# Causal attention scores two heads at a time in the two halves of the array's rows

## What is computed

```python
# second layer, attention: 16 heads of 8, no mask
scores = jnp.einsum('bhqd,bhkd->bhqk', q, k) / jnp.sqrt(jnp.float32(HEAD))
attn = jax.nn.softmax(scores, axis=-1)
ctx = jnp.einsum('bhqk,bhkd->bhqd', attn, v)
# second layer, inside its feed-forward part: 16 heads of 4, causal
q = _rope(split(c @ wq), pos)
k = _rope(split(c @ wk), pos)
scores = jnp.einsum('bhqd,bhkd->bhqk', q, k) / jnp.sqrt(jnp.float32(HD))
causal = jnp.tril(jnp.ones((s, s), bool))
scores = jnp.where(causal, scores, -jnp.inf)
attn = jax.nn.softmax(scores, axis=-1)
o = jnp.einsum('bhqk,bhkd->bhqd', attn, v)
```

## Time and profile before

| what | value |
|---|---|
| median of 3 runs | 2163.86 us (2159.7 to 2165.2) |
| the profiled execution's own time | 2163.9 us |
| its span, first to last instruction | 2162.0 us |
| PE busy | 2038.4 us, 94% |
| DVE busy | 1485.4 us, 69% |
| ACT busy | 1215.9 us, 56% |
| POOL busy | 294.9 us, 14% |
| granted clock of PE, mean | 0.968 |

### The profile page before, as it was taken

How to read it: one execution, slowest core, us unless ns; L and a number is a source line. 1 busy time by engine, 2 the same in 40 slices (tenths; PEclk the granted TensorE clock), 3 DMA queues, 4 the chain that set the end, 5 groups by cost and what they waited for, 6 DMA issues and landing times.

```text
span 2162.0 us, 33753 instructions
## 1 busy us (share of the span) xinstructions
PE 2038.4 (94%) x11936; PEld 944.3 (44%) x11936; DVE 1485.4 (69%) x2679; ACT 1215.9 (56%) x2325; POOL 294.9 (14%) x379
## 2 busy tenths in 40 slices
PE   7869999999999999998999999999999999999799
PEld 4522333436655233344665423343565633334355
DVE  5678887747686887664867788774677688777132
ACT  3224777774432677776451467777443267777621
POOL 2000011100033000110023200110003400011034
PEclk9957999999999999999999999999999999999989
DMA  5160101102171100001136010010117110100011
GB/s 193 35 175 1 31 16 29 29 2 61 50 204 30 30 16 26 17 17 32 50 110 143 11 31 16 27 31 2 56 48 189 48 34 3 31 17 16 2 49 40
DMA packets 66632, 105.17 MB, mean 49 GB/s; under 512 B 11136, under 2 KB 20288, under 8 KB 66080
## 3 DMA queue, kind: packets, MB, share of 16 engines
q1 hardware_dynamic: 66464, 103.03, 17.6%
HBM read 79.26 MB, written 22.94 MB: 47 GB/s over the span
## 4 chain that ended last, share of the span: by engine, by line
PE 83%; DVE 5%; ACT 3%; DMA 2%; issue 2%; POOL 1%; SPq 1%; POOLq 0%; DVEq 0%; ACTq 0%
PE ps L1692 19%; PE ps L1667 17%; PE ps L1636 16%; PE ps L1552 7%; PE ps L1587 6%; PE ps L1577 6%; DVE row_max L1202 3%; PE ps L1702 2%; ACT prob L1398 1%; DMA q_stack<-scratch_q 1%; PE ps L1509 1%; PE ps L1497 1%; PE ps L1669 1%; PE ps L1475 1%; PE ps L1503 1%
## 5 line engine op out<-in xcount | busy, mean ns | idle before, releaser
L1398 ACT ACTIVATE prob<-ps 128x512 f32<-128x512 f32 (+3 forms) x1792 | 869.1, 555 | 349.1 <-PE ps L1667 258.8
L1202 DVE TENSOR_REDUCE row_max<-ps 128x1 f32<-128x1024 f32 x512 | 606.7, 1220 | 123.3 <-PE ps L1636 121.4
L1667 PE MATMUL ps<-q_stack,k_stack 96*128 96x512 bf16 (+4 forms) x1792 | 557.9, 363 | 23.0 <-ACT prob L1398 17.0
L1636 PE MATMUL ps<-k_stack,q_stack 96*128 96x512 bf16 (+4 forms) x1792 | 535.6, 373 | 23.4 <-DMA q_stack<-scratch_q 12.0
L1199 DVE CUSTOM_DVE_ANT_0 tmp<-ps,const_b 128x128 f32<-128x128 f32 (+7 forms) x512 | 371.5, 756 | 131.2 <-PE ps L1636 117.7
L1692 PE MATMUL ps<-prob,v_ones 128*32 128x512 f32 (+3 forms) x3584 | 437.1, 560 | 2.5 <-ACT prob L1398 2.5
L1667 PEld LDWEIGHTS ps<-q_stack,k_stack 96*128 96x128 bf16 (+1 forms) x1792 | 172.7, 98 | 370.5 <-ACT prob L1398 246.0
L1636 PEld LDWEIGHTS ps<-k_stack,q_stack 96*128 96x128 bf16 (+1 forms) x1792 | 154.6, 99 | 370.1 <-DVE row_max L1199 94.9
L918 POOL TENSOR_TENSOR prob<-prob,spread_w 128x512 f32<-128x512 f32 x128 | 164.5, 1286 | 689.8 <-DVE prob L1086 511.7
L1552 PEld LDWEIGHTS ps<-wd,prob 128*128 128x128 f32 (+1 forms) x1600 | 208.0, 193 | 75.4 <-issue 53.4
L1345 ACT ACTIVATE prob<-ps 128x512 f32<-128x512 f32 x128 | 76.3, 596 | 284.2 <-PE ps L1577 275.8
(11 more groups left out here) (170 smaller groups left out, 1552.8 us busy)
## 6 DMA issues: line engine op xcount, KB each, us to landing
spread_w<-scratch_r SPq DMA_DIRECT2D x128, 128.0 KB, 2.9
spread_w<-scratch_r SPq DMA_DIRECT2D x64, 256.0 KB, 3.3
k_stack<-scratch_k SPq DMA_DIRECT2D x48, 256.0 KB, 6.8
q_stack<-scratch_q SPq DMA_DIRECT2D x48, 256.0 KB, 7.6
scratch_k<-tmp SPq DMA_DIRECT2D x36, 256.0 KB, 2.6
k_stack<-scratch_k SPq DMA_DIRECT2D x96, 64.0 KB, 2.2
q_stack<-scratch_q SPq DMA_DIRECT2D x96, 64.0 KB, 2.2
scratch_k<-tmp SPq DMA_DIRECT2D x36, 128.0 KB, 7.6
```

The lines of the kernel that those rows point to most:

```text
L1202: dve.tensor_reduce(nm[G % 2][:, t, j:j + 1], ring_pair(r)[:], AX_X, ALU.max).then_inc(s["ring_used"], 1)
L1398: act.activation(p_slot(v, j)[:, lo - at:hi - at], bank(UNIT_BANKS[u % 3])[:, 0:hi - lo], ACT.Exp, scale=SCALES[kind_of(G)]).then_inc(s["p ...
L1636: ins = pe.matmul(ring_pair(r)[:, lo:hi], queries(G, j)[:, t * P:(t + 1) * P], keys(G, j)[:, lo:hi], start=True, stop=True)
L1667: ins = pe.matmul(dst[:, 0:hi - lo], keys(G, j)[:, kc * P:(kc + 1) * P], queries(G, j)[:, lo:hi], start=True, stop=True)
```

## The change

Causal heads are multiplied over their own 48 rows (`of_head`), even heads in rows 0 to 47 and odd ones in rows 64 to 111, for queries and for keys. What follows from it:

- A causal piece holds a pair of heads (0 and 1, or 2 and 3), each in its own bank, and at most 512 keys of each; a tile with more keys makes two pieces. So a group has 24 pieces. DVE reduces both heads in one plain TENSOR_REDUCE; the maxima of the second piece go to `nmax_late` and are joined once a group, on which POOL's `maxima` waits (`max_joined`). The mask of the diagonal is now added on PE, by `hide`: matmuls of 64 rows and 64 columns, two for each head.
- Units of 256 or 128 queries hold two heads of the same half, side by side in one bank, and one exponential takes both. So a causal group has 40 units.
- Two units of heads of different halves are issued together where the planner has two banks free (`together`); they then wait for the exponential before the last instead of the second before the last.
- The mask of a unit is two `hide` matmuls of 64 rows and 64 columns for each head, in place of one of 128 rows and 128 columns.
- The buffers need no clearing: the memsets of `k_stack` and `clear_q` are gone, and the waits of `stack_in` on them.
- The planner has new costs and new pieces and units, and it may hold back a causal unit that could go only alone (`ALONE`). The value products are as before.

```diff
+    return [((j, j + 1), t, lo, min((t + 1) * P, lo + HALF)) for j in range(0, GH, 2) for t in range(T) for lo in range(0, (t + 1) * P, HALF)]
...
+def units_of(kind, q):
+
+    half, kc, lo, hi = QUADS[kind][q]
+    return [(0, 2), (1, 3)] if kind and hi - lo <= HALF // 2 else [(j,) for j in range(GH)]
...
-                pe += 0.03 + (hi - lo) * 1.82e-3
+                pe += 0.19 + (hi - lo) * 1.7e-3
...
             def piece(r, G, i):
-                j, t, n = PIECES[kind_of(G)][i]
+                heads, t, first, end = PIECES[kind_of(G)][i]
...
+                    dst = [ring_pair(r)[:, n * HALF:(n + 1) * HALF] for n in range(2)]
+                    for n, j in enumerate(heads):
+                        ins = pe.matmul(dst[n][:, 0:end - first], queries(G, j)[:, t * P:(t + 1) * P], keys(G, j)[:, first:end], start=True, stop=True)
+                    if end == (t + 1) * P:
+                        for half in range(2):
+                            for n in range(2):
+                                ins = hide(dst[n][:, t * P - first:end - first], n, piece_masks, half)
...
+            def hide(dst, odd, masks, half):
+
+                rows = slice(P // 2 * odd, P // 2 * (odd + 1))
+                return pe.matmul(dst[:, P // 2 * half:P // 2 * (half + 1)], masks[half != odd][rows, :], ident_b[rows, rows],
+                                 start=False, stop=True, skip_group_check=True)
...
-            def unit(u, G, q, j):
+            def unit(u, G, q, j, together):
...
+                count = 2 if together else 1
+                if u + count > 3:
+                    pe.wait_ge(s["p_ready"], u + count - 3)
+                dst = [bank(UNIT_BANKS[(u + n) % 3]) for n in range(count)]
+                heads = units_of(kind_of(G), q)[j:j + count]
+                blocks = [(n, k, heads[n][k], slice(k * (hi - lo), (k + 1) * (hi - lo))) for k in range(len(heads[0])) for n in range(count)]
+                ins = [None] * count
+                for n, k, head, to in blocks:
+                    ins[n] = pe.matmul(dst[n][:, to], keys(G, head)[:, kc * P:(kc + 1) * P], queries(G, head)[:, lo:hi], start=k == 0, stop=True,
+                                       skip_group_check=k > 0)
+                if kind_of(G) == 1 and lo == kc * P:
+                    for part in range(2):
+                        for n, k, head, to in blocks:
+                            ins[n] = hide(dst[n][:, to], head % 2, unit_masks, part)
```

More of the change, by code:

```diff
@@ L171, in windows @@
         stream = [(G, i) for G in range(first + 1, end) for i in range(len(PIECES[kind_of(G)]))]
-        units = [(G, q, j) for G in range(first, end) for q in range(len(QUADS[kind_of(G)])) for j in range(GH)]
+        units = [(G, q, j) for G in range(first, end) for q in range(len(QUADS[kind_of(G)]))
+                 for j in range(len(units_of(kind_of(G), q)))]
         quads = [(G, q) for G in range(first, end) for q in range(len(QUADS[kind_of(G)]))]
@@ L204, in windows @@
             can = [what for what, at in starts.items() if at <= soon]
+            both = "unit" in can and kind_of(units[0][0]) == 1 and units[0][2] % 2 == 0 and exped[-2] + LAT <= soon
+            if len(can) > 1 and "unit" in can and kind_of(units[0][0]) == 1 and units[0][2] % 2 == 0 and not both and act - pe > ALONE:
+                can.remove("unit")
             if "turn" in can:
@@ L220, in windows @@
                     self.add("stage_v", G + 1)
-                self.add("unit", self.units, G, q, j)
-                self.units += 1
-                pe += unit_time(hi - lo + (P if kind and lo == kc * P else 0))
+                heads = units_of(kind, q)
+                many = len(heads[0])
+                pe += many * (unit_time(hi - lo) + (0.08 if kind and lo == kc * P else 0.0))
                 at = quads.index((G, q))
-                act = max(act, pe + LAT, values_end[at - 2] + LAT if at >= 2 else 0.0) + 0.16 + (hi - lo) * 0.86e-3
-                exped.append(act)
-                if j == GH - 1:
+                for n in range(1 + both):
+                    j = units.pop(0)[2]
+                    self.add("unit", self.units, G, q, j, both + n if both else 0)
+                    self.units += 1
+                    act = max(act, pe + LAT, values_end[at - 2] + LAT if at >= 2 else 0.0) + 0.2 + many * (hi - lo) * 0.78e-3
+                    exped.append(act)
+                if j == len(heads) - 1:
                     exp_end[G, q] = act
@@ L237, in windows @@
                 if G == end - 1:
-                    done += 1
-                    n = GH * len(QUADS[kind])
+                    done += 1 + both
+                    n = sum(len(units_of(kind, q)) for q in range(len(QUADS[kind])))
                     while beside < len(late) * done // n:
@@ L717, in build, with causal_before @@
         ROUTED = [tuple(how) for what, *how in items if what == "routes_out"]
+        def causal_before(G):
+            return len([g for g in range(G) if kind_of(g) == 1])
         def routed_before(b, which):
@@ L926, in _ @@
                     stage_v(*how)
-                elif what == "stack_in" and kind_of(how[0]) == 1:
-                    clear_q(*how)
         @block.vector
@@ L1389, in before, with unit @@
                     part_of(2, int(stage[-1]), b)
[L1391 to L1392 removed]
+            def unit(u, G, q, n, together):
+                v, heads = QUAD0[G] + q, units_of(kind_of(G), q)[n]
                 half, kc, lo, hi = QUADS[kind_of(G)][q]
@@ L1662, in unit @@
                         pe.wait_ge(s["y_used"], HALVES[batch_of(G)])
[L1663 to L1670 removed]
+                if together == 2:
+                    return
+                count = 2 if together else 1
[12 more added lines that the diff above has]
+                            ins[n] = hide(dst[n][:, to], head % 2, unit_masks, part)
+                for n in range(count):
+                    ins[n].then_inc(s["st_psum"], 1)
             HALVES = {}
@@ L1676, in _ @@
                     halves += 1
-                elif what == "unit" and how[2:] == [0, 0]:
+                elif what == "unit" and how[2:4] == [0, 0]:
                     HALVES[batch_of(how[1])] = HALVES.get(batch_of(how[1]), halves)
```

101 lines of the change are left out of this document (50 added, 51 removed).

## The result

The changed kernel takes 2143.8 us in the median of 4 runs (2138.0 to 2144.4), against 2162.9 (2159.7 to 2165.2) for the kernel before in the same session: a ratio of 0.9907, 95% interval 0.9885 to 0.9929, or 19 us less. The forecast was 2135, and the range 2104 to 2180 holds the time. The profiled execution of the changed kernel took 2138.0 us, its shortest run, so the two traces are 25.8 us apart, some 7 us more than the medians. Within a kernel the time goes with the clock that PE was granted: the changed kernel took 2138.0 us at a mean clock of 0.968, and 2143.4 to 2144.4 us at 0.962 to 0.964.

The account below looks back on a forecast made before the run. PE bounds the kernel, with ACT's work and gaps a close second bound in causal groups. Causal groups gain 10.5 us a batch, groups 1 to 3 lose 3.3: 7.2 a batch, 29 in all, 2163.9 - 29 = 2135 us, range 2104 to 2180.

Parts of the forecast that it names:

- The halves overlap: Causal products in opposite row halves of PE run at once: 61.9 us saved in pieces, 28.0 in units.
- the ledger: Sum of PE's terms over the kernel: -89.9 overlap, +7.1 masks, +33.5 changes of mode, so -49 us.
- Masks: On PE, 512 large masks go and 2048 of 64 columns come, 0.027 us each, overlapping in pairs: net +7.1 us.
- Changes of mode: PE switching between whole array and halves costs 0.10 us each, 335 more changes, mostly in G = 3: +33.5 us.
- POOL and SP at nothing: 16 clears of 3.5 us and their waits go, but PE does not wait for these loads: no gain.
- The cap of a causal group: ACT's work and gaps hold causal groups at 26.5 us: G = 4 and 5 gain 3.7, G = 6 2.2.
- ACT's gaps unchanged: ACT's pauses between quads in the last group stay as before, 5.4 us of gaps a causal group.
- ACT -0.9 a group: Eight exponentials fewer in a causal group's narrow quads save ACT 0.9 us, bounds 0.4 and 1.4.
- 1: Rival: the halves do not overlap, PE has 62 us more: 2226 us, 9%.
- 2: Rival: masks of 64 columns have a floor of 0.053 us each on PE: 2189 us, 8%.
- 3: Rival: paired units wait for ACT, its gaps grow and the gain is lost: 2150 to 2172 us, 11%.
- 4: Rival: single units overlap too and gaps shrink, so all 49 us on PE arrive: 2114 us, 14%.

Follow-up runs that it names:

- experiment 1: The changed kernel with both heads of a causal piece in the same half, so nothing in a piece can overlap: 2200.9 us.
- experiment 3: The changed kernel with every mask of 64 rows and 64 columns issued twice, 2048 more: 2165.0 us.
- experiment 4: The changed kernel with the planner's cost of values set back to the old 0.03 + 1.82e-3 per column: 2133.5 us.
- experiment 5: The kernel before with only the planner's new cost of values, 0.19 + 1.7e-3 per column: 2169.7 us.
- experiment 2: The changed kernel in the same order, but units issued together no longer wait for two banks at once, each for its own: 2149.0 us.
- experiment 6: The changed kernel with a planner that never takes two units together nor holds one back: 2159.4 us.
- experiment 10: The changed kernel with one head in every unit, also in narrow quads, so no shared bank: 2186.5 us.
- experiment 9: The changed kernel again, unaltered, for its spread: 2146.7 us.
- experiment 11: The kernel of experiment 6 with the wide products of G = 7 issued twice in three batches: 2163.6 us.
- experiment 12: The kernel of experiment 8 with the wide products of G = 7 issued twice in three batches: 2139.7 us.
- experiment 8: The changed kernel with the old cost of values and a planner that gathers causal pieces for fewer changes of mode: 2128.2 us.

## Why the prediction was right, and where it was off

**The halves overlap: right, in full.** 3 ns between starts, and experiment 1 takes 57 us away with the overlap of the pieces, where the ledger had 61.9 and the masks of the pieces came on top, less what slack takes. The Trainium skill, "TensorE: Matmul & The Clock Gate", section "Measured speedup vs the span model", has 3.07 times for four row tiles; by the estimate that the prediction made from its share PE's sum would have been -22 us. PE's busy time fell by 46.1 us, and the ledger said 49. So for two halves, fed one after the other, this trace does not agree with the smaller share. Not all of the ledger came where it was put: in G = 4 and 5 PE's busy time fell by 4.5 and 3.5 us a batch, where the prediction had 5.5 and 4.2. No run tells which term was too high there.

**Masks: right.** 0.013 each (experiment 3), which is what the ledger took for masks in pairs, 0.027 for two.

**Changes of mode: right, 0.10 us.** G = 3 of the first batch takes 46.8 us, just under the 47 to 48 of the prediction. That G = 1 to 3 together hit the +13.2 with +14.1 is luck: G = 1 and 2 carry 7.4 of it, G = 1 with no more changes of mode in the first batch than before (32). Experiments 4 and 5 show that its loss, and 10 us of the total, hang on the planner's cost of values. The prediction read the changes of order out of the built program and never asked which edit had made them, so it did not see that the change carries an edit that works against it.

**POOL and SP at nothing: right; DVE not quite.** POOL is busy 66 us less, and PE waits for it nowhere in the windows of the first batch. DVE is busy 24.86 of 28.0 us in G = 5 now, 89% of the shorter stretch, and PE waits for it there (below).

**The cap of a causal group: right in kind, off in size.** The step that failed is the sentence "a causal group can't fall below ACT's work and the gaps: 22.0 - 0.9 + 5.4 = 26.5", in three places:
- G = 5, the largest miss (6 of the 10 us). The sum took the larger of two bounds, PE's 25.7 and ACT's 26.5. PE is busy 26.46 us now, and the stretch takes 28.0: PE stands idle for 1.5 us (0.3 before). G = 4 (PE 24.96, stretch 26.9) misses by less, 2.2 us over four batches, and in G = 6, with PE at 22.59, the cap holds: 26.6. PE's waits in G = 5 of the changed kernel (us in total, times, longest):

```profile
PE ps L1714 <- ACT prob L1426: 0.8, 3, 0.4
PE ps L1753 <- DVE row_max L1223: 0.3, 1, 0.3
```

  That two bounds which come near each other add up would be one reading. Experiment 1 speaks against it as the whole answer: there PE is busy 29.70 us in G = 5, 3.2 over ACT's 26.5, and still idles for 1.5 us, by the profile 1.3 of it for DVE. So PE idles in G = 5 for two engines, DVE being one that the prediction put at nothing. How the 1.5 us divide was not tested.
- "ACT's gaps unchanged" did not hold: 0.49 to 0.59 instead of 0.33 to 0.44 in wide quads, from the order that pairs bring (experiments 2 and 6).
- The term "ACT -0.9 a group" was mis-sized. ACT's busy time in the last group did fall by 0.94 (21.03 to 20.09), but the shared banks of the narrow quads are worth 1.9 us a group on average and 2.3 in the last (experiment 10), since turns go too, and PE's time with them. These two errors cancel in G = 6 and leave the last group 0.3 us better than its 0.9.

**G = 7** gains 2.2 instead of 3.6 us. PE is at its lower level for 20.5 us there over four batches, against 6.8 before, which the prediction took as unchanged; in the last batch, at full clock both times, the group gains its 0.9 and a little more. The same holds for the total. The changed kernel's median belongs to a clock of 0.963, while the kernel before was profiled at 0.968 and ran at 0.964 to 0.970 beside experiments 9 to 12; the two traces, both at 0.968, are 25.8 us apart against the 29 that were forecast. So of the 9 us between 2135 and 2143.8 about 6 come with the clock.

**The rivals.** 1 falls by experiment 1, 2 by experiment 3, the mechanism of 3 by experiment 2, though gaps did grow. 4, the whole ledger, did not come, but a better order comes nearer to it: 2128 us in experiment 8, 36 of the ledger's 49 us.

## What to carry to other kernels

Split a change that also retunes a scheduler's constants: run the scheduler's part alone, in the kernel before as well as without it in the changed one; here one constant hid a third of the gain. When a bound is lifted off a stretch, do not expect the next one to take over at its own value: here 1.5 us of waits for two engines stood on top, one of them an engine that looked free (DVE, 23.35 of 30.2 us before). An instruction merged out of a short chain of product, exponential and product can be worth more than its busy time, since its turn in the chain goes too. And before two medians are compared, compare the granted clock of their runs; in the changed kernel 0.01 of it was worth 11 to 15 us.

## What the runs showed of the hardware

- Two matmuls over 48 rows in different halves of the array, into different banks, start 3 ns apart and cost the time of one.
- A change between matmuls over the whole array and in the halves costs 0.10 us each way (0.312 and 0.319 against 0.216 us between starts); into the column quarters of the values it costs 0.09.
- PE's clock can stay at its lower level through 20 to 34 us in which PE is busy nearly without a break (20.02 of 20.50, 26.72 of 27.20 us), in stretches of units over 48 rows, masks over 64 and values over 128; the longest, 33.13 of 34.10 us, was in G = 6 and 7 of experiment 1. Within the windows of the kernel before such periods last 3.4 or 6.8 us. The longest of every kernel, 68 to 75 us, begins ahead of the first windows and ends in their first group, and PE has less to do in it. Of the kernel before:

```profile
116.90:188.60 71.70, 47.10 (x109) 9.97 (x107) 56.54 (x51) 11.34 (x14) 1.82 (x7) 0.50 0.46 111
```

  In one execution of a kernel a long period in G = 6 or 7 occurs and in another not. What decides it stays open.
